# A two-layer gated transformer block on one core: the router of a batch is run one batch step later

## What is computed

```python
x = x + tanh(g_xattn[0]) * L0_xattn(layernorm(x), ctx)   # 16-head attention, a null key/value, layer norm
x = x + tanh(g_ffn[0])   * L0_ffn(layernorm(x))          # relu, fp8-quantized hidden
x = x + tanh(g_xattn[1]) * L1_xattn(layernorm(x), ctx, lens)  # rmsnorm, W_in, decayed scan over patches
x = x + tanh(g_ffn[1])   * L1_ffn(layernorm(x))          # mixture of 8 experts, the best 2
# L1_ffn: logits = rmsnorm(x)*scale/16 @ router_w; softmax; top 2; weights renormalized;
#         out = sum over the 2 experts of weight * (gelu(x g0) * (x g1)) @ linear_w
```

## Time and profile before

| | |
|---|---|
| median of 3 runs | 1825.58 us (1823.18 to 1827.15) |
| span of the profiled execution | 1821.2 us |
| PE busy | 1535.9 us (84%) |
| DVE busy | 1215.9 us (67%) |
| ACT busy | 926.7 us (51%) |
| POOL busy | 593.8 us (33%) |
| mean granted TensorE clock | 0.952 |
| ranks of step 1, of step 14, of step 16 | 211.3, 1221.3, 1347.8 us |

### The profile page before, as it was taken

How to read it: one execution, slowest core, us unless ns; L and a number is a source line. 1 busy time by engine, 2 the same in 40 slices (tenths; PEclk the granted TensorE clock), 3 DMA queues, 4 the chain that set the end, 5 groups by cost and what they waited for, 6 DMA issues and landing times. The chain is left out here.

```text
span 1821.2 us, 39683 instructions
## 1 busy us (share of the span) xinstructions
PE 1535.9 (84%) x12540; PEld 1095.8 (60%) x12541; DVE 1215.9 (67%) x3316; ACT 926.7 (51%) x2530; POOL 593.8 (33%) x777
## 2 busy tenths in 40 slices
PE   3899999989989989998998999996628888888884
PEld 2667676676766767676675766765514544454452
DVE  6478888778887878878787887887433433334332
ACT  4477675666657657565665657666202222222221
POOL 3102323333232332423333232332332444444442
PEclk9899999999999999999999999998768999999997
DMA  8101202021020210203012020113006222222224
GB/s 236 58 2 59 70 2 71 13 61 65 7 72 3 69 45 29 70 2 72 13 59 66 7 71 2 52 48 111 30 16 207 45 42 46 43 43 46 41 45 119
DMA packets 78180, 98.39 MB, mean 54 GB/s; under 512 B 20576, under 2 KB 61680, under 8 KB 77936
## 3 DMA queue, kind: packets, MB, share of 16 engines
q1 hardware_dynamic: 51152, 77.01, 13.5%
q0 software_dynamic: 15872, 18.95, 6.5%
q10 hardware_dynamic: 10976, 0.13, 0.3%
HBM read 65.02 MB, written 35.23 MB: 55 GB/s over the span
## 5 line engine op out<-in xcount | busy, mean ns | idle before, releaser
L810 ACT ACTIVATE prob<-S,nm 128x256 f32<-128x256 f32 x512 | 235.5, 475 | 70.9 <-DVE nm L1506 67.6
L803 ACT ACTIVATE pTh<-T 128x512 f16<-128x512 f32 x256 | 139.3, 597 | 148.6 <-PE T L984 148.3
L1503 DVE TENSOR_REDUCE mx<-S 128x2 f32<-128x512 f32 x256 | 163.3, 679 | 39.9 <-PE S L1057 23.7
L1312 PE MATMUL S<-GL,xgh 128*128 x576 | 174.0, 384 | 10.6 <-issue 9.0
L654 POOL TENSOR_SCALAR ve_ln<-mv_ln 128x2 f32<-128x2 f32 x64 | 14.6, 228 | 484.6 <-DVE mv_ln L1477 484.1
L1515 DVE SCALAR_TENSOR_TENSOR pTl<-T,pTh 128x512 f16<-128x512 f32 x256 | 164.0, 681 | 3.4 <-ACT pTh L803 3.4
L819 ACT ACTIVATE prob<-prob,rden 128x256 f32<-128x256 f32 x256 | 116.3, 503 | 58.5 <-DVE p0n L1524 58.5
L725 POOL DMA_INDIRECT xg<-x_rows,trow x72 | 70.4, 977 | 228.2 <-DMA acc_rows<-ysb,yid 120.8
L984 PE MATMUL T<-ident,prob 128*128 128x128 f32 x1024 | 142.1, 283 | 1.5 <-DVE prob L1528 1.4
L979 PE MATMUL W<-cTh,Wkh 128*128 128x256 f16 x512 | 140.4, 274 | 0.0
L980 PE MATMUL W<-cTl,Wkh 128*128 128x256 f16 x512 | 140.4, 274 | 0.0
(11 more groups left out here) (296 smaller groups left out, 4534.9 us busy)
## 6 DMA issues: line engine op xcount, KB each, us to landing
cx<-in_ctx_dram SPq DMA_DIRECT2D x16, 512.0 KB, 5.4
gst<-in_L_ffn_gating_w_dram SPq DMA_DIRECT2D x16, 512.0 KB
gating_split<-gsp SPq DMA_DIRECT2D x16, 512.0 KB, 2.9
GL<-gating_split SPq DMA_DIRECT2D x8, 1024.0 KB, 5.2
stg<-in_L_xattn_Wkv_dram SPq DMA_DIRECT2D x8, 512.0 KB, 13.5
xl<-in_x_dram SPq DMA_DIRECT2D x16, 256.0 KB, 4.3
lst<-in_L_ffn_linear_w_dram SPq DMA_DIRECT2D x16, 256.0 KB
xres<-in_x_dram SPq DMA_DIRECT2D x16, 256.0 KB
```

The source lines that it names most:

```text
L803: A(flat(pTh[:, h, :, :]), T[h][:, :], ACT.Copy).then_inc(s_pTh[h], 1)
L810: ins = A(prob[:, h, t, :], S[h][:, t * NTOK:(t + 1) * NTOK], ACT.Exp, bias=nm[:, h, t:t + 1], scale=SM, accum_out=rs[:, h, t:t + 1])
L1312: ins = M(o[:, :], (xgl if n == 2 else xgh)[r % 2][:, k, :], GLflat[:, bass.ds(w, HID)], start=(k == 0 and n == 0), stop=(k == KD - 1 and ...
L1503: ins = V.tensor_reduce(mx[:, h, :], S[h][:, :].rearrange("p (t k) -> p t k", t=TT), AX.X, ALU.max)
```

## The change

The router becomes a fourth part, ROUTE, which works on batch i-2 in step i. Its pieces stand at other places of the step: PE's transposes at the end of j=0 (behind `wout`), its logits at the end of j=1, its ranks at the end of j=3; ACT's copy at j=1 and its exponential at j=4; DVE's `select` at j=2 ahead of the second k unit's low half, `take_ranks` and `place` at j=4 behind `ffn_out`. POOL's 4 transfers stay last in its step. The wait for the previous transfers goes from POOL to DVE's `place`. Steps 2 and 3 now stand written out ahead of the loop, which runs 10 steps and not 12, and a step 17 with ROUTE alone is added. Since UNITS has a new order, the banks behind position 3 are others.

```diff
 UNITS = [("p0T", False, POST), ("ctxT", True, PRE), ("ctxT", True, PRE), ("wout", False, POST),
-         ("xT", True, PRE), ("k", True, PRE), ("q", True, PRE), ("q", True, PRE),
+         ("x4T", False, ROUTE),
+         ("xT", True, PRE), ("k", True, PRE), ("q", True, PRE), ("q", True, PRE), ("logits", False, ROUTE),
          ("k", True, PRE), ("x1T", True, POST), ("q", True, PRE), ("q", True, PRE), ("s0", False, PRE),
          ("w1", False, POST), ("w1", False, POST), ("w1", False, POST), ("w1", False, POST), ("count", False, POST),
+         ("rank", False, ROUTE),
...
-         ("v", True, PRE), ("v", True, PRE), ("x4T", False, POST), ("logits", False, POST),
-         ("gT", True, ATTN), ("gT", True, ATTN), ("rank", False, POST)]
+         ("v", True, PRE), ("v", True, PRE),
+         ("gT", True, ATTN), ("gT", True, ATTN)]
-LOOP_START, LOOP_STEPS = 2, NB - 4
+LOOP_START, LOOP_STEPS = 4, NB - 6
...
# POOL
-                    for c in range(TT * TOPK):
-                        wait_apart(pool, s_scat[c], 16 * post.n)
                     rstd_of("lno", post, 1e-6 * WS * WS).then_inc(s_rstd["lno"], 1)
...
-                if POST in parts:
-                    wait_apart(pool, s_rec, post.n + 1)
+                if ROUTE in parts:
+                    wait_apart(pool, s_rec, routed.n + 1)
# DVE
                 def place():
+                    for c in range(TT * TOPK):
+                        wait_apart(dve, s_scat[c], 16 * routed.n)
...
                     if j == 2:
+                        if route:
+                            select()
                         if pre:
                             k_low(1)
...
                             ffn_out()
+                        if route:
+                            take_ranks()
+                            place()
```

More of the change, by code:

```diff
@@ L123, in end @@
     def end(self, step, parts):
-        if len(parts) == 3:
+        if len(parts) == 4:
             assert self.local == self.per, ("steps of a full batch step:", self.local)
@@ L470, in all_steps @@
             step(Batch(0, 1), {PRE, ATTN, POST})
+            for n in range(2, LOOP_START):
+                step(Batch(n // 2, n % 2), {PRE, ATTN, POST, ROUTE})
             for c in counts:
@@ L473, in all_steps @@
             with eng.Fori(0, LOOP_STEPS // 2) as t:
-                step(Batch(t + LOOP_START // 2, 0), {PRE, ATTN, POST})
-                step(Batch(t + LOOP_START // 2, 1), {PRE, ATTN, POST})
+                step(Batch(t + LOOP_START // 2, 0), {PRE, ATTN, POST, ROUTE})
+                step(Batch(t + LOOP_START // 2, 1), {PRE, ATTN, POST, ROUTE})
             for c in counts:
                 c.leave_loop()
-            for n in range(LOOP_START + LOOP_STEPS, NB + 1):
-                step(Batch(n // 2, n % 2), ({PRE} if n < NB - 1 else set()) | ({ATTN} if n < NB else set()) | {POST})
+            for n in range(LOOP_START + LOOP_STEPS, NB + 2):
+                step(Batch(n // 2, n % 2), ({PRE} if n < NB - 1 else set()) | ({ATTN} if n < NB else set())
+                     | ({POST} if n < NB + 1 else set()) | {ROUTE})
         def wait_apart(eng, sem, value):
@@ L643, in step @@
                 own.begin(i.n)
-                nxt, post = i.shift(1), i.shift(-1)
+                nxt, post, routed = i.shift(1), i.shift(-1), i.shift(-2)
                 def link(ins):
@@ L840, in step @@
                         prob_high(j - 1)
+                    if j == 1 and route:
+                        whole("x4T", flat(x4T[:, :, :]))
                     if j == 1 and pre:
@@ L893, in step @@
                     if j == 4:
+                        if route:
+                            act.wait_ge(s_dl, routed.n + 1)
+                            A(wk[:, :, 1:2], dl[:, :, :], ACT.Exp).then_inc(s_e1, 1)
                         if pre:
@@ L922, in step @@
                             v_high(3)
-                        if post_:
-                            whole("x4T", flat(x4T[:, :, :]))
                         if attn:
@@ L1208, in rank_unit @@
                 def rank_unit():
-                    pe.wait_ge(s_ms, post.n + 1)
+                    pe.wait_ge(s_ms, routed.n + 1)
                     o, s = bank("rank")
@@ L1233, in step @@
                             wout_unit()
+                        if route:
+                            rows_T("x4T", x4, (s_nrm["ln4"], routed.n + 1))
                     if j == 1 and pre:
@@ L1261, in step @@
                         q_unit(1)
+                    if j == 1 and route:
+                        logits_unit()
                     if j == 2:
@@ L1272, in step @@
                         count_unit()
+                    if j == 3 and route:
+                        rank_unit()
                     if j == 4 and post_:
@@ L1590, in select @@
                 def select():
-                    dve.wait_ge(s_rms, post.n + 1)
+                    dve.wait_ge(s_rms, routed.n + 1)
                     k, nfull, _ = work.at["logits"][0]
@@ L1636, in place @@
                     V.tensor_copy(slot[:, :], slotf[:, :]).then_inc(s_rec, 1)
[L1637 removed]
+                    dve.wait_ge(s_rec, routed.n + 1)
                 def q_low(m):
@@ L1747, in step @@
                             prob_low(j)
-                        if post_:
-                            select()
                         if attn:
@@ L1752, in step @@
                                 low("gT", m, gsp[:, 1, m, :], gsp[:, 0, m, :], WS)
-                        if post_:
-                            take_ranks()
                         if attn:
                             attn_low(3)
-                        if post_:
-                            place()
                 own.end(i.n, parts)
```

22 lines of the change are left out of this document (6 added, 16 removed).

## The result

The changed kernel takes 1885.9 us (median of 4 runs, 1879.1 to 1891.5) against 1826.1 us on the same chip: a ratio of 1.034, with a 95% interval of 1.031 to 1.036. It is slower by 60 us; the forecast was 1876 (1848 to 1910). The profiled execution spans 1877.3 us where that of before spans 1821.2, 56 us more.

A forecast was written before the change was run, and what follows sets the result against it. PE was taken to be busy nearly all of a step, with DVE nearly as full and in order. Steps +39, turns +5 and ends +5 make 49 on 1821.2 us, with 4.4 for the median 1876 us; range 1848 to 1910.

The forecast's parts named there:

- End of the step: From x4T's transposes to the next step's scores: 2.0 us shorter, with a new 1.3 us wait at values(7).
- Bank of the first k unit: At j=1 the k unit waits 2.4 us, not 0.95, until attn_out_scaled has read bank 0; stretch +1.4 us.
- select: DVE's select at j=2 delays the fourth q unit, with lateness at j=3: +1.3 us a step, bounds 0 and 2.7.
- take_ranks and place: At j=4 both stand on DVE's chain to xh, without slack: +2.2 us a step, bounds 1.9 and 2.6.
- A full step: Sum of the changes in a step with a router: +3.0 us, 79.5 us without a turn; 13 steps, +39 us.
- Loop turns: One of five goes, -3.3 us; the other four cost about 2 us more each, +8; sum +5, bounds -3 and +12.
- Ends: Step 1, step 15 and the drain, where place waits 4.5 us for batch 14's records to land: together +5 us.
- The clock rival: Half clock follows the new waits at the k unit and xh in every step, +32 us: 1908 us; 20%.
- Insertions partly covered: A later k unit gives DVE time; half of select and place hidden, a step costs 1.5 us: 1857 us; 14%.
- faster: DVE's 2 us earlier start carries through, freeing wout's bank by +2.1; a step loses 2.5 us: 1793 us; 6%.
- no change: The delays just eat the 2 us gained at the end of a step: 1826 us; 4%.
- the three delays: The k unit's bank at j=1, select, and take_ranks and place: sum 5 us; the change pays below 2 us.

The follow-up runs named there:

- before_loop10: The kernel before with steps 2 and 3 written out ahead of the loop, which then has ten steps as after the change: 1819.5 us (0.995).
- after_straight: The changed kernel with all of the loop's steps but two written out, so that it never turns: 1839.2 us (1.006).
- straight_three: after_straight with x4T's transposes behind the first k unit, select's rest at j=3 and place at the end of j=5: 1771.5 us (0.969).
- before_straight: The kernel before with all of the loop's steps but two written out, so that it never turns: 1785.2 us (0.977).
- straight_k_first: after_straight with x4T's transposes moved behind the first k unit, which changes that unit's bank: 1793.4 us (0.982).
- loop_k_first_place_end: The changed kernel, loop kept, with x4T's transposes behind the first k unit and place at the end of j=7: 1829.9 us (1.002).

## Why the prediction was right, and where it was not

The forecast was 1876 us, slower; it came out 10 us low, and in its range. (Its own terms sum to 1821.2 + 49 + 4.4 = 1874.6; it added 50.) The spans differ by 56 us where it had 49, and the median of after lies 8.6 us above the profiled span where it had allowed 4.4.

The starts of `scores(j)` on PE show how a step without a turn splits, from 443.68 us in before and from 617.82 in after:

| stretch | before | after | difference | forecast |
|---|---|---|---|---|
| scores(0) to (2): x4T, bank, logits | 19.6 | 20.6 | +1.1 | +1.4 |
| scores(2) to (4): select, ranks | 18.0 | 18.9 | +0.9 | +1.4 |
| scores(4) to (5) | 7.0 | 7.0 | 0 | 0 |
| scores(5) to (7): take_ranks, place | 18.1 | 20.3 | +2.2 | +2.2 |
| scores(7) to the next step | 13.8 | 11.6 | -2.2 | -2.0 |

(us; the differences are of the unrounded starts.)

*End of the step.* The wait for pTl at values(7) is 1.23 us, forecast 1.3, and `msel`'s is gone. The end got 2.2 us shorter, forecast 2.0. Right.

*Bank of the first k unit.* 2.17 us, forecast 2.4, and it was right that this is the largest single delay. The bank came free 4.45 us behind scores(1) (631.41 - 626.96), forecast 4.5. The forecast wait was 0.2 us long by a slip: its rows put the k unit at 3.29 - 0.95 = 2.3 us without its old wait, and not at 2.1. The stretch cost 1.1 us, forecast 1.4. The term was too small in what hangs on it: in straight code, where the wait is 2.26 us, half clock follows in most steps, and its removal was worth 4.1 us a step, in the loop 2.5, and not the 1.2 us by which I had it later.

*select.* q unit 4 waits 0.58 us for kl, forecast 0.85. Moving its rest gave 0.6 us a step, of a forecast 1.3. At j=3 DVE idles 2.9 us ahead of the boundaries, which takes up its lateness; what PE loses there is the ranks and 0.2 us of a longer wait for `hq` (0.79 for 0.58). With the ranks the stretch cost 0.9 us, forecast 1.4.

*take_ranks and place.* Forecast +2.2. The wait of values(4) is 1.49 us and that of xh rose by 0.58 (1.85 for 1.27), 2.1 in all; the stretch got 2.2 us longer. Right.

*A full step.* Forecast +3.0, 79.5 us; measured +2.0, 78.5 us, at the low end of what the text took for right. Two terms were too high, the k unit's stretch by 0.3 and select with the ranks by 0.5, and the end gave 0.2 more. By this term the sum was 13 us too high.

*Loop turns.* Here the sum failed. I had put +5 us for all of them, one gone and four dearer by 2 us; they cost about 16 us more, although the two steps written out are a gain by themselves (8 us in before_loop10). A turn went from 3.4 us on average to 8.0. I had only thought of the waits that a turn covers, and not that it could grow itself. Where DVE's place stands is worth 3.8 us a turn; through what, and where the rest comes from, stays open. By this term the sum was 11 us too low.

*Ends.* place of the last batch waited for the scatters, as forecast, but 2.9 us and not 4.5:

```profile
1405.67 0.19 DVE L1626 TENSOR_TENSOR pw<-oh,pes 128x32 f32<-128x32 f32 x1 [2.89 <-DMA routing_table<-rec,slot]
```

The ends came to some 2.5 us behind step 14, forecast 5.

*The clock rival (20%).* It had the right mechanism, at both places that I had named: half clock follows the k unit's wait and that for xh. But in the profiled execution it comes behind four of the ten waits of each kind in the loop, and not behind every one: 12 us over the steps at full clock, where the rival had 32 and the forecast nothing. In straight code it comes behind the k unit in 10 of 12 steps, and never behind xh, whose wait is 1.3 us there. In before it was free: the steps at 0.98, with half clock behind `msel`, last 76.5 us like the one at 1.00, and PE's wait for xn is gone from them. The Trainium skill's "TensorE: Matmul & The Clock Gate" (HAM oscillation) describes waits that recur once a round and leave PE cold each time. The traces agree in part: 0.50 stands behind the wait of 2.26 us in most steps of after_straight, but behind 2.17 and 1.85 us in after only now and then. Why a wait of the same length brings it in one step and not in the next, no run shows.

*Insertions partly covered (14%), faster (6%), no change (4%).* The first was right for select, whose price was halved. The second named the point from which the change pays: the three delays have to sum to less than 2 us. In straight_three, whose step is 1.0 us shorter than that of before_straight, they come to about 1 us by that count.

So the direction and the waits were forecast right: the end of the step, the bank and place are of the right size and place. That the total came out within 10 us is partly luck: the errors nearly cancelled, +13 for the steps and +2.5 for the ends against -11 for the turns and -12 for the clock.

## What to carry to other kernels

Where work units share a few banks in rotation, an inserted unit changes the bank of every unit behind it: for each of them look up who reads the bank it now gets, and how late; here that was 46 of 54 us in straight code, and a first repair that looked at one unit only made it 34 us worse. Put a moved block where its own engine idles, and check what waits right behind it: in straight code place cost the same at j=4 and at the end of the step, and less at j=5 (where it was measured only together with the other two edits). Before such moves, measure the loop itself, and compare kernels with the same loop: writing it out gave 43 us here, writing out two steps alone 8 us.

## What the runs showed of the hardware

A wait of 2.26 us brought PE down to 1.2 GHz for some 3.4 us in 10 of 12 steps of straight code. In the ten loop steps of after the one of 2.17 us did so four times and the one of 1.85 us four times. In straight_k_first, where no wait is above 1.3 us, PE stayed at 2.4 GHz in every full step. The price, 1.7 us, is nearly as much as the wait's; in the steps of before without a turn, where it follows the wait for `msel`, it cost nothing. The turn of a loop cost 3.3 us in the earlier trace rows, 6.0 in loop_k_first_place_end, and 8.5 to 10.7 us in the kernels where DVE stops 1.4 us behind PE, up to 1.3 us of that being half clock behind other waits. At full clock each step of the loop was 1.0 to 2.1 us longer than the same step written out.
